# Ten tables on chip with look-ups shared by two chunks, and pair products in short bursts: a recommendation tower on one core

## The reference

```
e = stack([tbl_f[ids[:, f]] for f in range(26)])       # 2048 x 26 x 128
combined = concatenate([dense[:, None, :], e])         # 2048 x 27 x 128
inter = einsum('bnd,bmd->bnm', combined, combined)[:, triu_i, triu_j]   # 351 pairs
z = concatenate([dense, inter, dense])
h = relu(z @ W_top1 + b1)      # 607 -> 512
h = relu(h @ W_top2 + b2)      # 512 -> 256
y = h @ W_top3                 # 256 -> 1
```

## Time and profile before

| | |
|---|---|
| median of 3 runs | 377.36 us (376.21 to 377.71) |
| profiled execution, span of its trace | 375.2 us |
| TensorE busy | 329.8 us (88%) |
| GpSimd busy | 258.0 us (69%) |
| VectorE busy | 198.1 us (53%) |
| ScalarE busy | 191.4 us (51%) |
| chain that ended last | PE 52%, POOL 25%, issue 12% |

### The profile page before, as it was taken

One profiled execution on the slowest core, in us unless ns is written; L12 is line 12 of the kernel. 1 busy time (PEld: TensorE's weight loads), 2 busy tenths in 40 slices (PEclk: granted clock), 3 DMA queues, 4 the chain that ended last, 5 costly groups with the idle time before them and its releaser, 6 DMA issues.

```text
span 375.2 us, 13452 instructions
## 1 busy us (share of the span) xinstructions
PE 329.8 (88%) x6048; PEld 297.8 (79%) x6048; DVE 198.1 (53%) x364; ACT 191.4 (51%) x234; POOL 258.0 (69%) x280
## 2 busy tenths in 40 slices
PE   0476856999989999999999999999899988999797
PEld 0475745998779978997799878997799867997586
DVE  3599741995049901993079704990099405940000
ACT  2587633456544655455444653465535563455323
POOL 6777777777777777777777777777777777774000
PEclk9998985999999999999999999999999999999969
DMA  6997492663236623662266324752266225423140
GB/s 158 258 260 183 119 317 55 140 207 90 51 91 148 199 52 76 141 211 63 61 141 198 92 59 96 191 145 59 70 149 196 73 54 127 112 56 71 35 67 2
DMA packets 55415, 45.72 MB, mean 122 GB/s; under 512 B 39444, under 2 KB 45179, under 8 KB 55359
## 3 DMA queue, kind: packets, MB, share of 16 engines
q1 hardware_dynamic: 45783, 26.91, 28.8%
q0 software_dynamic: 8704, 17.84, 18.0%
q10 hardware_dynamic: 871, 0.11, 0.2%
HBM read 37.91 MB, written 6.93 MB: 120 GB/s over the span
## 4 chain that ended last, share of the span: by engine, by line
PE 52%; POOL 25%; issue 12%; ACT 4%; DVE 3%; DMA 3%; ACTq 1%; SPq 0%; DVEq 0%
PE banks L441 27%; POOL rows L399 25%; PE banks L460 7%; PE mlp L479 6%; PE moved L424 5%; PE mlp L489 4%; PE mlp L520 2%; DVE masks L682 2%; DMA hot_ids<-in_ids_of_field_dram 1%; DMA rows<-in_tbl_dram,ids_sb 1%; ACT vectors L771 1%; DVE low L669 1%; ACT vectors L754 1%; PE banks L531 1%; PE mlp L500 1%
## 5 line engine op out<-in xcount | busy, mean ns | idle before, releaser
L399 POOL DMA_INDIRECT rows<-in_tbl_dram,ids_sb x272 | 257.1, 945 | 83.8 <-issue 81.1
L682 DVE TENSOR_TENSOR masks<-hot_ids,row_of 125x512 fp32r<-125x512 int32 (+1 forms) x336 | 181.5, 614 | 17.9 <-PE banks L441 13.4
L441 PE MATMUL banks<-masks,high 125*128 125x256 f32 x592 | 151.3, 295 | 18.9 <-DVE low L669 18.9
L441 PE MATMUL banks<-masks,low 125*128 125x256 f32 x592 | 146.9, 287 | 0.0
L441 PEld LDWEIGHTS banks<-masks,high 125*128 125x128 f32 x592 | 116.2, 196 | 20.9 <-issue 16.3
L441 PEld LDWEIGHTS banks<-masks,low 125*128 125x128 f32 x592 | 116.3, 196 | 0.1
L771 ACT ACTIVATE vectors<-moved 128x384 f32<-128x384 f32 (+1 forms) x80 | 87.8, 1097 | 3.9 <-PE moved L424 3.5
L754 ACT ACTIVATE vectors<-banks 128x512 f32<-128x512 f32 (+1 forms) x40 | 44.6, 1114 | 77.8 <-PE banks L441 77.8
L460 PEld LDWEIGHTS banks<-vectors 128*27 128x27 f32 x4096 | 45.6, 107 | 29.7 <-issue 23.1
L460 PE MATMUL banks<-vectors 128*27 128x27 f32 x4096 | 54.8, 196 | 14.5 <-issue 10.2
L691 DVE COPY vectors<-dense_sb 128x256 f32<-128x256 f32 x8 | 3.5, 435 | 103.1 <-PE banks L460 103.1
(11 more groups left out here) (33 smaller groups left out, 56.6 us busy)
## 6 DMA issues: line engine op xcount, KB each, us to landing
hot_ids<-in_ids_of_field_dram SPq DMA_DIRECT2D x32, 256.0 KB, 5.1
scratch<-products SPq DMA_DIRECT2D x28, 169.0 KB
rows<-in_tbl_dram,ids_sb POOLq DMA_INDIRECT x272
features<-scratch SPq DMA_DIRECT2D x7, 351.0 KB
w_sb<-in_tbl_dram SPq DMA_DIRECT2D x3, 448.0 KB
scratch<-products SPq DMA_DIRECT2D x28, 42.2 KB
dense_sb<-in_dense_dram SPq DMA_DIRECT2D x8, 128.0 KB, 4.8
hot_ids<-in_ids_of_field_dram SPq DMA_DIRECT2D x8, 128.0 KB
```

What stands on the lines that cost most here:

```text
L399: pool.indirect_dma_start(rows[:, (tile * TILE_ROWS + v) % RING, :], None, tables[f][:, :], bass.IndirectOffsetOnAxis(ap=ids_sb[:, tile, f ...
L441: last = nc.tensor.matmul(banks[:, j % BANKS, m * CHUNK:(m + 1) * CHUNK], part[:, part_of(j * PAIR + m, k), :], masks[:, mask % MASK_RING, ...
L682: nc.vector.tensor_tensor(masks[:, mask % MASK_RING, 0:size], hot_ids[0:PART_ROWS, n % ID_RING, 0:size], row_of[0:PART_ROWS, row:row + 1]. ...
```

## The change

One more long table is kept on chip (`LONGS` takes two, ten tables in all), so 16 tables are gathered for a tile instead of 17. The first chunk alone still gathers the two long ones: 2 x 18 + 14 x 16 = 260 gathers. The ring of gathered rows has 24 buffers instead of 34, and `vectors` room for four tiles.

A look-up now takes **one table for two neighbouring chunks** (a unit), so that `high` and `low` of a part are each multiplied by one mask of 512 columns: 2 matmuls for each mask. Five tables (the first set) join the chunks (1,2), (3,4), (5,6) and take 0 and 7 alone, the other five (the second set) join (0,1), (2,3), (4,5), (6,7); one table's first chunk is gathered. That makes 44 units with 368 masks: 284 of 512 columns and 84 of 256 (before 256 and 80). Look-ups have two banks `looked`, and the mask ring has 7 places.

The steps of `multiply` have two banks `crossed`, and a step is cut in **four bursts of 16 samples**, each behind one part of a look-up. In the turn of chunk p: two look-ups with the four steps of chunk p in them, three more look-ups (all five for chunks p+1 and p+2), then the layers of the same chunk p without products between them. The last chunk's four steps have no look-up left and stand nearly alone.

```diff
-LONGS = [f for f in range(FIELDS) if ROWS[f] == LONG][:1]
-ONE_HOT = [f for f in range(FIELDS) if ROWS[f] == SHORT] + LONGS
+LONGS = [f for f in range(FIELDS) if ROWS[f] == LONG][:2]
+SHORTS = [f for f in range(FIELDS) if ROWS[f] == SHORT]
+ONE_HOT = LONGS + SHORTS
...
+BURST_GROUPS = 4
+FIRST_SIZES, LATER_SIZES = (4, 4, 4, 3, 3), (4, 4, 4, 4)
+RING = 24
+TILE_SLOTS = 2 * TILES
+FIRST_SET, SECOND_SET = (2, 3, 4, 5, 1), (6, 7, 8, 9, 0)
...
+def chunks_of(k, h):
+    return [c for c in (k - 1, k) if 0 <= c < CHUNKS and (c > 0 or h >= len(LONGS))]
+UNITS = [(h, chunks_of(k, h)) for k in range(CHUNKS + 1) for h in set_of(k) if chunks_of(k, h)]
+COLUMNS = [len(chunks) * CHUNK for _, chunks in UNITS]
...
             sp.wait_ge(low_made, HOT)
...
-            load_dense(1)
-            for j in range(HOT_PAIRS):
-                load_hot_ids(1, j)
+            for u in units_of(2):
+                load_hot_ids(u)
+            def chunk(p):
+                u = units_of(p + 3) if p + 3 <= CHUNKS else [len(UNITS)] * len(FIRST_SET)
+                load_hot_ids(u[0])
+                load_dense(p + 2)
+                load_hot_ids(u[1])
+                write_products(p)
+                store_y(p - 1)
+                load_pairs(p)
+                load_hot_ids(u[2])
...
+            def look_up(u, ks=None):
+                h, _ = UNITS[u]
+                ks = ks or range(PARTS[h])
+                if ks[0] == 0:
+                    pe.wait_ge(low_made, TABLES.index(h) + 1)
+                    if u >= 2:
+                        pe.wait_ge(unit_kept, u - 1)
+                for k in ks:
+                    mask = FIRST_MASK[u] + k
+                    pe.wait_ge(mask_made, mask + 1)
+                    for part in (high, low):
+                        last = nc.tensor.matmul(looked[:, u % 2, 0:COLUMNS[u]], part[:, part_of(h, k), :],
+                                                masks[:, mask % MASK_RING, 0:COLUMNS[u]],
...
+            def multiply(c, s, groups=range(STEP_GROUPS)):
+                n = c * CHUNK_STEPS + s
...
+                if s == TILE_STEPS and groups[0] == 0:
+                    pe.wait_ge(batch_kept, batches_before(TILES * c + 2))
+                if n >= 2 and groups[0] == 0:
+                    pe.wait_ge(step_kept, n - 1)
...
+            def look_up_and_multiply(u, parts, c, s):
+                for n in range(STEP_GROUPS // BURST_GROUPS):
+                    look_up(u, [parts[n]])
+                    multiply(c, s, range(n * BURST_GROUPS, (n + 1) * BURST_GROUPS))
...
+            def chunk(p):
+                b_now, a_next, b_next = TILES * p + 1, TILES * (p + 1), TILES * (p + 1) + 1
+                u = units_of(p + 2)
+                look_up_and_multiply(u[0], range(0, 4), p, 0)
                 turn(b_now, 2)
+                look_up_and_multiply(u[0], range(4, 8), p, 1)
                 turn(b_now, 3)
+                last_layer(p - 1)
+                look_up_and_multiply(u[1], range(0, 4), p, 2)
+                look_up_and_multiply(u[1], range(4, 8), p, 3)
                 turn(a_next, 0)
+                look_up(u[2])
                 turn(a_next, 1)
+                look_up(u[3])
+                turn(a_next, 2)
+                look_up(u[4])
+                turn(a_next, 3)
+                first_layer(p, 0)
+                first_layer(p, 1)
+                turn(b_next, 0)
+                first_layer(p, 2)
+                first_layer(p, 3)
+                second_layer(p, 0)
+                turn(b_next, 1)
+                second_layer(p, 1)
+            def last_chunk():
+                b_now = TILES * LAST + 1
                 multiply(LAST, 0)
+                turn(b_now, 2)
                 multiply(LAST, 1)
+                last_layer(LAST - 1)
                 turn(b_now, 3)
                 multiply(LAST, 2)
                 multiply(LAST, 3)
...
+            def keep_unit(u):
+                h, chunks = UNITS[u]
+                if chunks[-1] >= 2:
+                    act.wait_ge(step_ready, (chunks[-1] - 1) * CHUNK_STEPS)
```

650 lines of the change are left out of this document (297 added, 353 removed).

## The result

The changed kernel takes **424.7 us** (median of 4 runs, 422.3 to 425.7) against 377.5 us, a ratio of 1.1244 with a 95% interval of 1.1192 to 1.1296: slower, as forecast, but by 21 us more than the 403.5 us and outside the range. Its profiled execution has a span of 423.8 us. Further down, where runs of one kernel lay 1.5% or more above its fastest, the ratio leaves them out and the median does not, so the ratio is what to compare there.

| | forecast | measured |
|---|---|---|
| start, until the turn of chunk 1 begins | 105.6 | 114.7 |
| five turns | 220.0 | 231.7 |
| turn of chunk 6 | 41.9 | 44.1 |
| last chunk, until the layers of its first half | 15.0 | 16.4 |
| layers of the two halves | 18.8 | 16.9 |

A forecast was written before the change was run, and what follows sets the result against it. TensorE was taken to bound the kernel, GpSimd nearly level before. Start 105.6, five turns at 44.0, chunk 6 41.9, last steps 4.3, memory way 10.7, layers 18.8: span 401.3, plus 2.2 gives 403.5 us; range 384 to 420.

The forecast's parts named there:

- Bounds: Before, TensorE and GpSimd nearly level; after, TensorE's turn 44.0 us, with GpSimd's 40 us of gathers below that pace.
- Look-ups: In a chunk's turn on TensorE, 84 matmuls of 512 columns at 0.216 us: 18.1 us, +0.3; bounds 18.1 to 20.2.
- Steps: In a chunk's turn on TensorE, 16 bursts at 0.44 us: 7.0 us instead of 7.4, -0.4.
- Waits: New TensorE waits per turn: look-up bank 1.3, turned batch 0.8, masks 1.2, second layer 0.7; 4.0 us; products' way nothing.
- A turn: A middle chunk's time on TensorE: 40.3 us of work plus 4.0 of waits, 44.3, taken as 44.0.
- The turns of batches: In a chunk's turn on TensorE, 8 turns with 32 tables instead of 10 with 34: -0.4 us.
- The start: VectorE splits tables until 57.2 us; TensorE stands 59.5 to 68.0 for unit 9's ids, 2.5 for low clock; ends at 105.6.
- The end: Chunk 6's turn 41.9 us, last chunk's steps 0 and 1 4.3, first half's way through memory 10.7, halves' layers 18.8.
- Rival 3: In the steps, bursts run as slow as whole steps: 22 us more, 425 us; chance 10%.
- Rival 4: The clock falls in each turn, 2.5 us lost in each of six: 15 us more, 418 us; chance 7%.
- Rivals 1 and 2: First: gathers bound, turn at most 40 us, 361 us, 5%. Second: waits melt in turns and start, 384 us, 13%.

The follow-up runs named there:

- e3_two_halves: Changed kernel with each 512-column mask multiplied as two halves of 256 columns, same weights: 428.4 us, ratio 1.1344 to the kernel before.
- e1_ids_first: Changed kernel with unit 9's ids fetched ahead of the wait for the layers' weights: 416.5 us, ratio 1.1019 to the kernel before.
- e12_read_behind_writes: Changed kernel with all edits together, layers fed the chunk before's products, read back behind the writes: 395.9 us, ratio 1.0487 to the kernel before.
- e2_whole_steps: Changed kernel with each step whole behind its four look-up parts instead of cut in four bursts: 418.2 us (412.6 to 421.8), no ratio.

## Why the prediction was right in direction and wrong in size

- **Bounds.** Right: TensorE bounds the turn, GpSimd waits.
- **Look-ups, mis-sized.** Two ends stood open, 0.216 and 0.24; I took the lower on the ground that a shared weight load must win. Measured 0.233: 84 x 0.017 = 1.4 us a turn, and 568 x 0.017 = 10 us in the kernel. e3_two_halves shows that there was next to nothing to share. The 131 ns of the Trainium skill ("TensorE: Matmul & The Clock Gate", Back-to-back issue gap) were not seen in any run here; the measured spacing is 1.8 times that.
- **Steps, the term that failed.** 0.44 for a burst counted the change up to the start of the next large matmul (0.09 and 0.12) and not the 0.11 us by which that matmul's own record is longer, with its weights' loading in it. Measured 0.547: 16 x 0.107 = 1.7 us a turn, and so "-0.4 for the steps" became +1.3. In seven chunks it is 12 us; without this error, or without that of the look-ups, the time would have stayed in the range. The earlier trace rows could not show it: there the next instruction behind a step was a turn. Another place of that trace shows such a price: behind the last layer's matmuls, with weights one column wide, the first look-up matmul of 256 columns takes 0.22 us to the next start, where 0.12 is usual.

```profile
194.06 0.39 PE L441 MATMUL banks<-masks,high 125*128 125x256 f32 x1
194.28 0.28 PE L441 MATMUL banks<-masks,low 125*128 125x256 f32 x1
```

- **Waits, near in sum, with parts that offset one another.** 4.0 forecast, 3.5 found in the turn shown: 1.05 for the bank (1.3), 0.37 for the batch (0.8), 0.23 for masks (1.2; the fifth look-up's 20 large matmuls took 4.89 us, 20 x 0.233 are 4.66), 0.73 for the second layer (0.7), and 1.15 for the products, put at nothing with the remark that a smaller wait for masks would be paid there. It was: the way took 242.53 - 226.41 = 16.1 us (15.7 forecast), TensorE's 15.0.
- **A turn.** 40.3 + 1.7 + 1.4 + 3.5 = 46.9, and 46.3 was measured. The 0.6 are not accounted for term by term. The turns of batches do not give them: they took 3.7 us in the 40.8 of before and take 3.4 beside their waits here, 0.3 less where 0.4 was forecast. The 40.8 held a step that took 2.38 us to the next start where the other three took 1.74 to 1.79, which would be as much.
- **The start, mis-sized.** The mechanism was there, with its place and its release (e1_ids_first took it away). The ten tables were split at 61.3, not 57.2: until then VectorE waited 7.9 us for ScalarE and 1.0 for TensorE, where 4 had been put without a row. The ids came 11.9 us later, not 10.4. Eight parts took 10.5 us, not 9.5; beside 8 x 1.013 that leaves 2.4 for the low clock (2.5 forecast), so the 1.0 is the bursts'. Steps 2 and 3 ended at 84.5 (77.5). Then a term was miscounted: in chunk 0 these two steps stand on one look-up and not on two, so four look-ups with 34 parts follow, and not three with 26. 8 parts more are 3.7 us, most of the waits that were put there did not come, and the layers began 18.3 us behind the steps, not 15.6. They took 11.9, not 12.5.
- **The end.** Chunk 6's turn: 15.3 us until its steps were done (13.3), 14.5 for the products' way (14.1), 14.3 from there (12.0 and 2.5 for the clock). The last chunk took 16.4 and not 15.0, with stops of 1.9 and 2.7 us inside its steps that the forecast did not have.
- **Rival 3** gave the right time, 425, for the wrong reason: it had a burst at 0.63 by the pace of the small matmuls. They kept the quick pace; the change was dear. Its 22 us met the sum of 12 for the bursts and of other errors by luck. **Rival 4** did not come: the two longest stops of a turn, 1.05 and 1.15 us in the one shown, left the clock at 1.00. **Rivals 1 and 2** needed 40 to 42 us a turn, which even e12_read_behind_writes does not reach.

The range should have had the upper end of both open prices at once: 0.24 for the large matmuls and 0.63 for the bursts make 403.5 + 7 x (2.1 + 3.0) = 439, and I let 420 stand.

## What to carry to other kernels

Count a change between full-array and narrow matmuls in both directions, the second one inside the record of the large matmul behind it: read starts, over a whole period. Where two prices lie open in the same direction, let the range take both. Count the first and the last round of a loop from the program, not from the middle ones. And before a wait for a transfer is taken away by moving the transfer, look at what runs under its new place.

## What the runs showed of the hardware

- The look-ups' matmuls (4-byte data, rounded, with a weight load each): 0.233 us apart for 512 columns, 0.12 for 256 (and e3_two_halves). Half the columns took half the time with as many loads per matmul, so the columns set the pace here, not the loads. The layers' records, also of 256 columns, are 0.216 apart.
- 32 records of small matmuls start within 0.233 us (0.0075 each), 64 within 0.55; in whole steps of e2_whole_steps the 81st starts at 1.0 us and the 128th at 1.63 (medians over 22 steps), stops included.
- TensorE's stops inside rows of small matmuls, ended by nothing that the profile shows: 2.4 us under the weights' loading, about 2 us some 4 to 6 us behind the issue of a 351 KB read, gone when that read was moved. A large read is not needed: in the changed kernel's last chunk, with all four steps nearly side by side, there is one of 1.9 us before 394.8, where 392 to 396 us show 8 GB/s, all of it on an instruction queue. That instructions are fetched late fits, and was not shown.
- The clock's windows show 0.50 to 0.59 behind stops of 9.6, 5.9, 2.4 and 1.7 + 0.8 us, and 1.00 behind two of 0.8 and 1.0 us that were 14 us apart (idle times as the profile gives them). They also show 1.00 behind stops of 1.9 and 1.3 us in the changed kernel's last chunk (394.8 to 402.7), so the length of a stop alone did not decide it.
